# Attention weights summed as three bf16 parts, with a 32-wide and a 196-wide one-hot in place of two fp32 ones

## What is computed

```python
alpha = leaky_relu(s_src[row] + s_dst[col], negative_slope=0.2)   # 4 heads
ex = exp(alpha - m[row])
alpha_n = ex / denom[row]
msg = alpha_n[:, :, None] * h[col]
out = segment_sum(msg, col, num_segments=N)
```

## Time and profile before

| | us |
|---|---|
| median of three runs | 5283.91 |
| the profiled execution | 5286.63 |
| its span, first to last instruction | 5284.7 |
| PE, DVE, ACT, POOL busy in the span | 4093.3, 3801.5, 2968.5, 3140.3 |
| softmax stage, tail (first of the 1664-element subtractions to last Exp) | 2448.7 to 2473.5 |
| weights stage (first DVE operation to end of the copy of `acc`) | 2474.16 to 3056.21 |

### The profile page before, as it was taken

How to read it: one execution, slowest core, us unless ns; L and a number is a source line. 1 busy time by engine, 2 the same in 40 slices (tenths; PEclk the granted TensorE clock), 3 DMA queues, 4 the chain that set the end, 5 groups by cost and what they waited for, 6 DMA issues and landing times. The chain is left out here.

```text
span 5284.7 us, 99383 instructions
## 1 busy us (share of the span) xinstructions
PE 4093.3 (77%) x24366; PEld 3419.4 (65%) x24367; DVE 3801.5 (72%) x8168; ACT 2968.5 (56%) x4399; POOL 3140.3 (59%) x3290
## 2 busy tenths in 40 slices
PE   6888887887888888302999977777777777777778
PEld 5776776776676666202999936666666666666666
DVE  9866666666666666369999957777777777777776
ACT  4455555555555555204777756666666666666665
POOL 0277777777777777710000007777777777777774
PEclk9998888888989889656999989999999999999999
DMA  9854555555555544892000076666666666666665
GB/s 387 273 139 132 131 133 130 131 134 129 133 131 134 129 133 132 116 66 63 0 0 0 0 189 146 145 145 145 148 145 145 145 145 147 146 145 145 145 147 134
DMA packets 1157486, 695.20 MB, mean 132 GB/s; under 512 B 923563, under 2 KB 974949, under 8 KB 1157325
## 3 DMA queue, kind: packets, MB, share of 16 engines
q1 hardware_dynamic: 807980, 307.66, 29.9%
q0 software_dynamic: 131424, 275.52, 17.9%
q10 hardware_dynamic: 218048, 111.65, 7.3%
HBM read 542.65 MB, written 145.42 MB: 130 GB/s over the span
## 5 line engine op out<-in xcount | busy, mean ns | idle before, releaser
L1122 POOL DMA_INDIRECT g_q<-q_d,g_aux x1660 | 1572.4, 947 | 1385.1 <-DMA pw<-g_q 879.5
L613 POOL DMA_INDIRECT rec_d<-rec,place x1568 | 1514.4, 966 | 490.3 <-issue 475.9
L1429 PE MATMUL g_hp<-pw,g_mix 128*128 x3328 | 879.9, 387 | 309.8 <-ACT g_mix L1326 304.8
L1440 PE MATMUL g_ap<-g_hid,g_oh 128*128 128x256 f32 x3328 | 878.4, 386 | 141.3 <-DVE agg L1232 138.1
L720 PE MATMUL lk<-tab_sd,low 128*128 128x196 f32 x3136 | 976.6, 396 | 0.0
L1346 ACT ACTIVATE g_hid<-g_q 128x512 f32<-128x512 f32 x832 | 523.9, 630 | 712.6 <-DVE g_q L1218 701.4
L1218 DVE TENSOR_TENSOR g_q<-g_hp,g_q 128x512 f32<-128x512 f32 x832 | 573.2, 689 | 486.2 <-DMA g_q<-q_d,g_aux 344.4
L1429 PEld LDWEIGHTS g_hp<-pw,g_mix 128*128 128x128 f32 x3328 | 618.6, 191 | 468.0 <-issue 391.5
L592 ACT ACTIVATE equal<-rk,minus_two 128x512 bf16<-128x512 f32 x392 | 259.3, 685 | 943.1 <-DMA rec_d<-rec,place 704.0
L1440 PEld LDWEIGHTS g_ap<-g_hid,g_oh 128*128 128x128 f32 x3328 | 597.6, 190 | 288.7 <-issue 219.1
L1232 DVE TENSOR_TENSOR agg<-agg,g_ap 128x256 f32 x1664 | 689.1, 414 | 99.8 <-PE g_ap L1440 36.4
(11 more groups left out here) (256 smaller groups left out, 5115.1 us busy)
## 6 DMA issues: line engine op xcount, KB each, us to landing
low_row<-rows_d SPq DMA_DIRECT2D x392, 256.0 KB
g_ea<-rec_d SPq DMA_DIRECT2D x208, 256.0 KB, 3.6
rec<-in_ea ACTq DMA_DIRECT2D x196, 256.0 KB
rec_d<-pad ACTq DMA_DIRECT2D x49, 936.0 KB, 6.7
hx_row<-rows_d SPq DMA_DIRECT2D x392, 98.0 KB
g_lrow<-low_row_d SPq DMA_DIRECT2D x208, 128.0 KB, 4.4
g_q<-q_d,g_aux POOLq DMA_INDIRECT x1660, 3.0
rec_d<-rec,place POOLq DMA_INDIRECT x1568
```

Source lines behind the costliest of these rows:

```text
L613: pool.indirect_dma_start(rec_d, bass.IndirectOffsetOnAxis(ap=place[0:n, at, j:j + 1], axis=0), rec[0:n, at, j, :], None).then_inc(s_sc[at ...
L1122: pool.indirect_dma_start(qg[:, par, j, :], None, q_d, bass.IndirectOffsetOnAxis(ap=aux[:, par, j, F_IDX - F_LOW:REC - F_LOW].bitcast(I32) ...
L1429: mm = pe.matmul(hp[u][:, k * HID:(k + 1) * HID], mix[:, par, 2 * u + k, :], pw[:, bass.ds(b[k], 1), :].rearrange("p o f -> p (o f)"), sta ...
L1440: mm = pe.matmul(ap[u % 2][:, k * HID:(k + 1) * HID], oh[:, par, 2 * u + k, :], hid[:, u, k, :], start=True, stop=True)
```

## The change

Each weight is split exactly into three bf16 parts: w1 = bf16(w), w2 = bf16(w - w1), w3 = w - w1 - w2. The destination is now cut at 32: a low part below 32 (`QTR`) and a high part below 196 (`NQ`). PE's stationary side is the low one-hot (32 wide) times the weights of four heads, 128 columns for each of the three parts (`spread`); its moving side is the high one-hot, 196 columns of bf16, and three matmuls a tile add into the same bank. The result lies as [head x 32, 196] and is turned into `wgt` by 16 copies of 32 x 49 (`quarters`), 8 on DVE and 8 on ACT. ACT now makes half of the high one-hots (196 wide), DVE the other half and all low ones. The high digits that DVE reads lie twice side by side (`high_two`); every operand of its three operations is bf16. In the softmax stage ACT writes `high_two`, and the first two parts of the weights, DVE the remainders and the third part; `ORDER` interleaves them with the last head's work.

The core of the diff (left out: the layout of the tiles in `pw`, the new cut of the digits, `ORDER` (the two kinds of step in the order in which DVE takes them) and a constant's semaphore):

```diff
@@ -52,6 +52,7 @@
 FILL = 26
 ROW_STEP = (NODES_P - P) // FILL
 HF = HEADS + 1
+QTR, NQ, THREE = 32, NODES_P // 32, 3
 HALF_ROW = 32
 HG = G // 2
 LK = HF * NB
...
@@ -752,7 +753,11 @@
         pw_flat = pw[:, :, :].rearrange("p b f -> p (b f)")
         agg_flat = agg[:, :, :].rearrange("p b f -> p (b f)")
         al, sc = (pw_flat[:, k * HEADS * S:(k + 1) * HEADS * S].rearrange("p (h s) -> p h s", h=HEADS) for k in range(2))
-        low_dst, high_dst, from_first, to_last, rest, low_in = (pw_flat[:, k * S:(k + 1) * S] for k in range(2 * HEADS, 2 * HEADS + 6))
+        rest, low_in, low_half, high_dst, from_first, to_last = (pw_flat[:, k * S:(k + 1) * S] for k in range(2 * HEADS, 2 * HEADS + 6))
+        halved_bf = low_half.bitcast(BF16)
+        low_dst = halved_bf[:, 0:S]
+        high_two = halved_bf[:, S:2 * S].rearrange("p (g j s) -> p g j s", j=HG, s=2)
+        thirds = pw_flat[:, HEADS * S:(2 * HEADS + 2) * S].bitcast(BF16).rearrange("p (k h s) -> p k h s", k=THREE, h=HEADS)
         fwd = pw_flat[:, (2 * HEADS + 6) * S:(2 * HEADS + 7) * S + 1]
         low_in = low_in.bitcast(I32)
         with ExitStack() as soft:
...
@@ -839,7 +846,11 @@
                         act.wait_ge(s_in[k], 16)
                         at = slice(k * SC, (k + 1) * SC)
                         act.activation(low_dst[:, at], fld[:, at, DLOW], ACT.Copy)
-                        act.activation(high_dst[:, at], fld[:, at, DHIGH], ACT.Copy).then_inc(s_ld, 1)
+                        act.activation(high_dst[:, at], fld[:, at, DHIGH], ACT.Copy)
+                        gs = slice(k * SC // G, (k + 1) * SC // G)
+                        by_group = fld[:, at, DHIGH].rearrange("p (g j) -> p g j", j=G)
+                        act.activation(high_two[:, gs, :, :], by_group[:, :, HG:G].unsqueeze(3).to_broadcast([P, SC // G, HG, 2]),
+                                       ACT.Copy).then_inc(s_ld, 1)
                     for h in range(HEADS):
                         act.wait_ge(s_mr, h + 1)
                         act.activation(line[h], al[:, h, :], ACT.Exp)
...
@@ -851,9 +862,21 @@
                         act.activation(line[h], sc[:, h, :], ACT.Ln, bias=tiny[:, 0:1]).then_inc(s_ln, 1)
                     act.wait_ge(s_dn, HEADS + 1)
                     act.activation(piece[:, :, :, :], piece[:, :, :, :], ACT.Ln, bias=tiny[:, 0:1]).then_inc(s_ln, 1)
-                    for h in range(HEADS):
-                        act.wait_ge(s_fin, h + 1)
-                        act.activation(al[:, h, :], al[:, h, :], ACT.Exp)
+                    def weight(h):
+                        act.wait_ge(s_fin, ORDER.index(("log", h)) + 1)
+                        act.activation(al[:, h, :], al[:, h, :], ACT.Exp).then_inc(s_exp, 1)
+                        act.wait_ge(s_exp, HEADS + 2 + h)
+                        act.activation(thirds[:, 0, h, :], al[:, h, :], ACT.Copy).then_inc(s_ln, 1)
+
+                    def second(h):
+                        act.wait_ge(s_fin, ORDER.index(("rest", h)) + 1)
+                        act.activation(thirds[:, 1, h, :], al[:, h, :], ACT.Copy).then_inc(s_mr, 1)
+
+                    for h in range(HEADS + 1):
+                        if h < HEADS:
+                            weight(h)
+                        if h:
+                            second(h - 1)
 
                 @block.vector
                 def _(v):
...
@@ -992,12 +1015,26 @@
                     link(v.tensor_tensor(piece[:, 0, :, :], piece[:, 1, :, :], piece[:, 0, :, :], ALU.subtract))
                     link(v.tensor_tensor(piece[:, 0, :, :], piece[:, 0, :, :], peak[:, 1, :, :], ALU.subtract))
                     link(v.tensor_scalar(piece[:, 0, 0, :], piece[:, 0, 0, :], one_run[:, 0:1], None, ALU.mult))
-                    for h in range(HEADS):
+                    def log_weight(h):
                         link(v.scalar_tensor_tensor(out=line[h], in0=from_first[:, :], scalar=piece[:, 0, 1, h:h + 1], in1=line[h],
                                                     op0=ALU.mult, op1=ALU.add))
                         link(v.scalar_tensor_tensor(out=line[h], in0=to_last[:, :], scalar=piece[:, 0, 0, h:h + 1], in1=line[h],
                                                     op0=ALU.mult, op1=ALU.add))
                         v.tensor_tensor(al[:, h, :], al[:, h, :], line[h], ALU.subtract).then_inc(s_fin, 1)
+
+                    def after_first(h):
+                        v.wait_ge(s_ln, HEADS + 2 + h)
+                        v.tensor_tensor(al[:, h, :], al[:, h, :], thirds[:, 0, h, :], ALU.subtract).then_inc(s_fin, 1)
+
+                    def after_second(h):
+                        v.wait_ge(s_mr, HEADS + 2 + h)
+                        v.tensor_tensor(thirds[:, 2, h, :], al[:, h, :], thirds[:, 1, h, :], ALU.subtract)
+
+                    for step, h in ORDER:
+                        (log_weight if step == "log" else after_first)(h)
+                        if step == "rest" and h:
+                            after_second(h - 1)
+                    after_second(HEADS - 1)
 
 
         w2 = sb("w2", [P, 2, D], F32)
...
@@ -1127,21 +1167,33 @@
                 gather(NGS - 2, 0)
                 gather(NGS - 1, 1)
 
+            def quarters(copy, h):
+                for q in range(HEADS):
+                    ins = copy(wgt[q * QTR:(q + 1) * QTR, h, :], acc[h * QTR:(h + 1) * QTR, q:NQ:HEADS])
+                return ins
+
             @block.vector
             def _(v):
                 def weigh(g, at):
-                    tile = lambda a: a[:, bass.ds(g * G, G)]
                     if not first(g, 4):
                         v.wait_ge(d_acc, g - 3)
-                    v.tensor_tensor(oh_high[:, at, :, :], col(tile(high_dst), P, G, NB), row(iota[:, 0:NB], P, G, NB),
-                                    ALU.is_equal).then_inc(d_hi, 1)
-                    v.tensor_tensor(oh_low[:, at, 0:HG, :], col(low_dst[:, bass.ds(g * G, HG)], P, HG, P),
-                                    row(iota[:, :], P, HG, P), ALU.is_equal)
+                    v.tensor_tensor(oh_low[:, at, :, :], row(low_dst[:, bass.ds(g * G, G)], P, QTR, G), low_of, ALU.is_equal
+                                    ).then_inc(d_hi, 1)
+                    v.tensor_tensor(oh_high[:, at, HG:G, :].rearrange("p j (a s) -> p j a s", s=2),
+                                    high_two[:, bass.ds(g, 1), :, :].rearrange("p o j s -> p (o j) s").unsqueeze(2)
+                                    .to_broadcast([P, HG, NQ // 2, 2]),
+                                    high_of.rearrange("p (a s) -> p a s", s=2).unsqueeze(1).to_broadcast([P, HG, NQ // 2, 2]),
+                                    ALU.is_equal)
                     v.wait_ge(d_hi, g + 1)
-                    v.tensor_tensor(oh_w[:, at, :, :, :], oh_high[:, at, :, :].unsqueeze(2).to_broadcast([P, G, HEADS, NB]),
-                                    al[:, :, bass.ds(g * G, G)].rearrange("p h j -> p j h")
-                                    .unsqueeze(3).to_broadcast([P, G, HEADS, NB]), ALU.mult).then_inc(d_w, 1)
-
+                    parts = thirds[:, :, :, bass.ds(g * G, G)].rearrange("p k h j -> p (k h) j")
+                    v.tensor_tensor(spread[:, at, :, :, :], row(oh_low[:, at, :, :].rearrange("p q j -> p (q j)"), P, THREE * HEADS, QTR * G)
+                                    .rearrange("p c (q j) -> p c q j", j=G),
+                                    parts.unsqueeze(2).to_broadcast([P, THREE * HEADS, QTR, G]), ALU.mult).then_inc(d_w, 1)
+
+                v.tensor_copy(low_of, col(iota[:, 0:QTR], P, QTR, G))
+                v.tensor_copy(high_of[:, 0:P], iota[:, :])
+                v.tensor_scalar(high_of[:, P:NQ], iota[:, 0:NQ - P], float(P), None, ALU.add).then_inc(s_const, 1)
+                v.wait_ge(s_const, 1)
                 quads(v, weigh, NGS)
                 link = Chain(v, s_nc)
                 v.memset(eps_col[:, :], EPS).then_inc(s_eps, 1)
...
@@ -1149,8 +1201,10 @@
                 v.wait_ge(s_par, 32)
                 v.wait_ge(s_hh, 16)
                 v.wait_ge(d_acc, NGS)
-                v.tensor_copy(wgt[:, :, :].rearrange("p h a -> p (h a)"), acc[:, 0:HEADS * NB]).then_inc(s_wg, 1)
-                v.wait_ge(s_wg, 1)
+                for h in range(2):
+                    ins = quarters(v.tensor_copy, h)
+                ins.then_inc(s_wg, 1)
+                v.wait_ge(s_wg, 2)
 
                 def add_messages(c):
                     bs, n = chunk[c], SIZES[c]
...
@@ -1271,17 +1325,21 @@
                 def turned_low(g, at):
                     if not first(g, 4):
                         act.wait_ge(d_acc, g - 3)
-                    for j in range(HG, G):
-                        ins = act.activation(oh_low[:, at, j, :], iota[:, :], ACT.Abs, bias=low_dst[:, bass.ds(g * G + j, 1)], scale=-1.0)
+                    for j in range(HG):
```

(30 more changed lines are left out.)

9 lines of the change are left out of this document (3 added, 6 removed).

## The result

The changed kernel takes 5210.17 us (median of four runs, 5209.96 to 5212.89), beside 5283.24 us (5281.72 to 5284.38) for the kernel before on the same chip: a ratio of 0.9863, 95% interval 0.985 to 0.9875. The forecast was 5213 us.

The account below looks back on a forecast made before the run. DVE was taken to bound the kernel before at 2.782 us a group, ACT the changed one at 2.38. Terms: -83.6 + 0.7 - 0.4 + 12.8 = -70.5 us, giving 5213 us against the median; 8-in-10 range 5195 to 5245.

Parts of the forecast that it names:

- The bound: Weights stage: ACT becomes the slowest engine at 2.38 us a group, from 2.782; over 208 groups -83.6 us.
- DVE: Weights stage: three bf16 operations, 0.200 + 0.475 + 1.667 = 2.34 us a group, from first-stage rows of 1600 and 4096 elements.
- The wait ahead of the product: DVE, weights stage: waiting for the 256-element operation costs nothing; 0.08 us more if it stopped the overlap.
- PE: Weights stage: 24 bf16 matmuls of 196 columns at 0.09 us, weight loads hidden, 2.16 us a group.
- the PE rival: Weights stage: two hand-overs of 0.16 us make PE the bound at 2.48 us a group, 5234 us; chance 0.11.
- Start and end: Weights stage: three small DVE tables at its start, +0.7 us; last matmuls and sixteen copies at its end, -0.4 us.
- Softmax stage: Eight more DVE operations of 1664 elements, 14.5 us, less the last Exp, 1.6; ACT's copies hidden: +12.8 us.
- The casts: Softmax stage: four ACT casts of the paired digits, hidden while ACT waits for loads; 2.9 us at most otherwise.
- Product at one element a cycle: Weights stage: DVE's 3072-element product takes 3.27 us, DVE 3.94 a group, 5538 us; chance 0.03.
- the other terms' 13.1 us: Added to the weights-stage change in rivals' prices; the terms beside the groups were start +0.7, end -0.4, softmax +12.8.
- Weight load open: Weights stage: up to 40 ns of each PE weight load exposed, 122 ns a matmul, 2.92 us a group, 5326 us; chance 0.03.
- The clock: Weights stage: PE's pauses lower the granted clock to 0.90, 2.59 us a group, 5257 us; chance 0.03.

Follow-up runs that it names:

- The two takings-away: Changed kernel without ACT's Relu in the weights stage: 5212.65 us; changed kernel with DVE's product cut to 2048 of 3072 elements, PE's work kept: 5219.21 us.
- PE alone: Changed kernel without ACT's Relu and with DVE's product over two parts, PE still making three matmuls a tile: 5149.16 us, ratio 0.9732.
- the first four experiments: Edits of the changed kernel: no Relu, 0.9851; product over two parts, 0.9865; both, 0.9732; an fp32 operand in the product, 1.0482.
- the second sitting: The changed kernel run again without edit, on another chip: 5210.31 us beside 5283.25 us for the kernel before.
- the kernels that end it at 2903.66 and 3196.80: Changed kernel without third parts, one more high one-hot on DVE: 5129.39 us; with a quarter of the product on POOL, same one-hot moved: 5418.77 us.

## Why the prediction was right

*The bound.* Right: ACT, at 2.385 us a group (forecast 2.38). The two takings-away prove it from both sides: without the Relu the stage falls to DVE's 2.348 us, with a shorter product nothing moves. The sum was right in its parts too: 68 columns more cost an Abs 54 ns (390 to 444; 57 by the line taken), 272 elements more the Relu 229 (722 to 951; 228).

*DVE.* Right: 2.357 us (2.34). From product to first operation 1.67 us (2697.80 to 2699.47 in the trace), then 0.20 and 0.48; the first stage's line, 0.067 us + 0.521 ns an element, held for a multiplication of 3072. The wait ahead of the product cost nothing.

*PE.* The term was mis-sized: 24 x 0.09 = 2.16 us, measured 2.02 with PE alone. The step that failed is "so 0.09 us with the load hidden". It was no error of reading: in the nanoseconds of the trace of before, the next start follows the count's 196-column matmul after 89 ns (the median of 196 of them). What failed is to carry that over. With PE alone five of six starts follow after 83 to 85 ns and every sixth after 88 to 90, 84.3 in the mean. The loads have one form in both places; the count's moving side is 49 columns read four times over, that of the weights stage 196 in a row. Whether this makes the 5 ns was not tested. The error did not reach the sum, since PE was not the bound; it did make the PE rival likelier than it was.

*Start and end.* Tables 0.57 us (0.7; the third has 68 elements, not 70); from the last Relu to the message product 3.27 us (3.1), with copies of 0.21 us each (0.2 taken).

*Softmax stage.* +12.80 us for +12.8: eight operations at their free pitch, less the last Exp, with ACT's copies hidden. That it fits so closely is in part luck, since the terms were rounded to 0.1. The casts were hidden too: from DVE's first operation in the stage (2293.86 before, 2294.51 after) to the first log step it is 154.87 and 154.86 us.

*The rivals.* PE as the bound by its hand-overs: when PE was the bound, none cost anything. Product at one element a cycle: its price was right (pitch 3.949 for 3.94), its condition not met; the operand's type is what decides. The limit at which this rival was said to decide, a product of 2.17 us, has the other terms' 13.1 us with the wrong sign: the change stops paying at 2.04 (2.782 - 13.1/208 - 0.675). Weight load open: 84.3 ns, not 122. The clock: 1.00 in the stage, and still 1.00 with PE idle for 43% of it. Its price was too high: at a mean clock of 0.90, 24 matmuls of 0.09 us take 2.16/0.9 = 2.40 us and not 2.59, which is 5217 us and hardly to be told from the forecast.

*What was missed.* "The gather stage behind it starts that much earlier and is otherwise untouched": the work was, its time was not. The parts that were forecast sum to -69.3 us in place of -70.5, the way up to the softmax tail took 0.6 more (ahead of the stage's first DVE operation), and -7.5 came from behind the stage: -76.2. The profiled execution of before lies 3.4 above its median. In which part those lie no trace tells: the code ahead of the tail scatters as well, and in the traces of the first four experiments, where it is the same, the first log step starts between 2446.38 and 2451.80. Between medians the change is worth 73.1 us, so about 4 remain that the forecast parts do not hold, and the second sitting shows them again (72.9). 4.4 of the 7.5 lie in the node products. The windows view of that stretch, before and after:

```profile
3056.00:3149.00 93.00, 66.18 (x151) 24.66 (x151) 49.94 (x171) 46.28 (x153) 0.00 (x0) 0.85 0.91 234
```

```profile
2987.50:3076.50 89.00, 64.96 (x151) 25.16 (x151) 50.20 (x171) 46.65 (x154) 0.00 (x0) 0.85 0.95 245
```

Counts of instructions, busy times and the mean clock are alike; the same transfers (0.91 x 93 and 0.95 x 89, 84.6 us of DMA both times) are packed closer. What decides how closely they pack stays open. The time at which the weights stage ends does not order it (the kernels that end it at 2903.66 and 3196.80 have nearly the same node products), and 4 us is less than half of what identical code showed from trace to trace. Against mere scatter stands that both sittings have them; whether the change itself moves the mean of what lies behind was not settled. The median came 2.8 us under the forecast because these 4 us outweigh the small misses, 1.2 and 0.6, on the other side; that the misses partly cancel is luck.

## What to carry to other kernels

Where several engines feed each other through deep buffers, sum each engine by itself from start-to-start pitches, and take the largest; then shorten each in turn, for a busy share near 100% on two engines names neither. A re-cut that doubles the elements can still be free if it brings every operand of the large operation to a type that runs at twice the rate, and one operand left in fp32 turns the gain of 1.4% into a loss of 4.8%. Before a resting POOL is given tensor work beside a full DVE, price what DVE loses while POOL runs: here 1.3 us a group for a quarter of a product.

## What was not expected of the hardware

- 768 bf16 products on POOL (1.66 us) stretch the 196-element operation that DVE starts meanwhile to 1.51 us in one form (0.25 without POOL) and to 1.56 in another, which was not run without POOL.
- A 128-column weight load and a 196-column bf16 matmul together take 84.3 ns in a stream: 83 to 85 five times, then 88 to 90 once.
- The granted clock stays at 1.00 over 400 us in which PE works only 57% of the time, with pauses of some 1.7 us in every group.
- Identical code behind the changed stage took 2220.9 to 2229.3 us in eleven traces, with the same instructions and the same transfers.
